# Quads of expert rows loaded and stored in 4 KB runs, and four shared units moved behind quads 5, 11, 17 and 23

## The reference

```
probs = softmax(x2 @ router_w + router_b)            # 64 experts
w, e  = top 8 of probs, weights divided by their sum
moe   = sum over k of w[k] * (silu(x2 @ w1[e[k]] + b1[e[k]]) @ w2[e[k]] + b2[e[k]])
share = sum over 2 shared experts of silu(x2 @ sw1 + sb1) @ sw2 + sb2
out   = layernorm(x2 + moe + share)
```

## Time and profile before

| | before |
|---|---|
| median of 3 runs | 1846.71 us |
| profiled execution: time, span | 1847.5 us, 1845.4 us |
| TensorE busy, mean granted clock | 88%, 0.94 of full |
| VectorE, ScalarE, GpSimd busy | 63%, 34%, 49% |
| chain that ended last | PE 61%, DVE 11%, POOL 11%, DMA 6% |
| quads in the trace | first load issued at 591.6 us, last store issued by 1023.9 us |
| transfers of a quad, time to landing | load 5.8 us, store 4.5 us (medians of 80) |

### The profile page before, as it was taken

How to read it: one execution, slowest core, us unless ns; L and a number is a source line. 1 busy time by engine, 2 the same in 40 slices (tenths; PEclk the granted TensorE clock), 3 DMA queues, 4 the chain that set the end, 5 groups by cost and what they waited for, 6 DMA issues and landing times.

```text
span 1845.4 us, 45541 instructions
## 1 busy us (share of the span) xinstructions
PE 1623.4 (88%) x17739; PEld 1302.6 (71%) x17739; DVE 1165.2 (63%) x3228; ACT 627.1 (34%) x957; POOL 897.3 (49%) x1000
## 2 busy tenths in 40 slices
PE   6898988887898999989998689899882999999994
PEld 5676767776665666766776457677662999999994
DVE  4577777776511776775567578888762445565564
ACT  1233333232311774545554344445421111111110
POOL 0007777777782008888888776533334003223223
PEclk9999999997999999999998799999985999999997
DMA  9516656556688898888889632211315113333332
GB/s 328 183 39 213 218 189 206 178 195 207 203 242 231 280 314 264 286 290 282 294 287 325 238 99 86 82 59 65 122 50 193 53 51 92 93 95 95 95 101 66
DMA packets 269202, 322.41 MB, mean 175 GB/s; under 512 B 25035, under 2 KB 245055, under 8 KB 268223
## 3 DMA queue, kind: packets, MB, share of 16 engines
q1 hardware_dynamic: 232671, 226.01, 38.6%
q0 software_dynamic: 33024, 92.32, 15.4%
q10 hardware_dynamic: 3296, 1.17, 0.3%
HBM read 157.02 MB, written 162.40 MB: 173 GB/s over the span
## 4 chain that ended last, share of the span: by engine, by line
PE 61%; DVE 11%; POOL 11%; DMA 6%; issue 5%; ACT 4%; SPq 1%; DVEq 0%; POOLq 0%; ACTq 0%
PE wide L2147 14%; PE d_yp L2159 7%; POOL big L1509 7%; PE wide L110 4%; PE wide L127 3%; PE wide L1261 3%; PE bank L1095 3%; PE bank L1281 3%; PE wide L1264 2%; PE wide L1248 2%; DMA e_x<-lists 2%; POOL rest_ones L253 2%; PE e_yp L1815 2%; PE bank L1274 2%; ACT pt L746 2%
## 5 line engine op out<-in xcount | busy, mean ns | idle before, releaser
L1509 POOL DMA_INDIRECT big<-results,slots x256 | 266.8, 1042 | 197.9 <-DMA results<-e_y 121.6
L2147 PE MATMUL wide<-d_xt,d_ws 128*128 128x128 f32 x2272 | 278.0, 276 | 0.6 <-issue 0.6
L2147 PEld LDWEIGHTS wide<-d_xt,d_ws 128*128 128x128 f32 x2272 | 271.7, 193 | 4.5 <-issue 1.0
L680 POOL DMA_INDIRECT lists<-big,slots x160 | 157.9, 987 | 84.5 <-DVE slots L1035 38.6
L746 ACT ACTIVATE pt<-wide 77x2048 f32<-77x2048 f32 x64 | 119.7, 1871 | 132.7 <-PE wide L1264 132.2
L2047 ACT ACTIVATE d_gate<-wide 128x512 f32<-128x512 f32 x71 | 42.4, 597 | 326.0 <-PE wide L2147 326.0
L2012 POOL DMA_INDIRECT d_picked<-results,slots x64 | 63.0, 984 | 179.6 <-DMA results<-d_y 166.4
L1524 DVE SCALAR_TENSOR_TENSOR big<-big,weights 128x256 f32<-128x256 f32 x256 | 111.0, 495 | 42.7 <-DMA big<-results,slots 25.3
L110 PE MATMUL wide<-shared_sx,shared_sw 128*128 128x512 f32 x256 | 127.7, 622 | 7.3 <-DMA shared_sx<-res_t 4.9
L2159 PE MATMUL d_yp<-d_wd,d_h 128*128 x568 | 134.2, 379 | 0.0
L127 PEld LDWEIGHTS wide<-shared_sw,shared_sh 128*128 128x128 f32 x512 | 98.8, 194 | 45.7 <-issue 30.1
(11 more groups left out here) (289 smaller groups left out, 3327.4 us busy)
## 6 DMA issues: line engine op xcount, KB each, us to landing
lists<-zero SPq DMA_DIRECT2D x20, 2048.0 KB, 14.7
e_x<-lists SPq DMA_DIRECT2D x80, 512.0 KB, 5.8
results<-e_y SPq DMA_DIRECT2D x80, 512.0 KB, 4.5
d_x<-lists SPq DMA_DIRECT2D x71, 128.0 KB, 2.2
results<-d_y SPq DMA_DIRECT2D x71, 128.0 KB, 1.7
e_w<-in_L_w SPq DMA_DIRECT2D x2, 4096.0 KB, 40.0
shared_sw<-in_x_t SPq DMA_DIRECT2D x32, 128.0 KB
x<-in_x SPq DMA_DIRECT2D x8, 512.0 KB
```

The lines of the kernel that those rows point to most:

```text
L680: pool.indirect_dma_start(out=lists, out_offset=bass.IndirectOffsetOnAxis(ap=slots[:, b, i, k:k + 1], axis=0), in_=z2[i % 3][:, b, :], in_ ...
L1509: pool.indirect_dma_start(out=picked[:, c % NG, b, :], out_offset=None, in_=results[0:-(-PAGES_OF_STEP[s] // 4) * 4 * R0, :], in_offset=ba ...
L2147: ins = mm(out[T % 2][:, a * P:(a + 1) * P], ws[:, T % NW, n, c, a * P:(a + 1) * P], xt[:, T % 2, c], start=c == 0, stop=c == KC - 1)
```

## The change

Three edits. First, `rows_of` lays a quad out so that partition p holds four rows that are neighbours in memory: one run of 4 KB in place of four of 1 KB. For that the integer places are permuted inside each quad, in five more small VectorE operations per step; the float places are kept in `weights` (whose values for the step are written only later), so `slot` and `slots_f` fall away. Second, 16 units instead of 20 stand ahead of the first quad (units 8 to 23). Third, units 24, 25, 26 and 27 follow one each behind quads 5, 11, 17 and 23. `PLANNED` counts the operations of a plan that lost one.

```diff
-        slot = sb("slot", [P, NB, K])
+        slot = None if first else sb("slot", [P, NB, K])
+        row = sb("row", [P, 3, NB, K], mybir.dt.uint32) if first else None
...
                         for b in range(NB):
-                            ins = nc.vector.max(slot[:, b], place[:, b])
+                            ins = nc.vector.max(weights[:, b, i, :], place[:, b])
                         step(ins)
+                        step(nc.vector.tensor_copy(row[:, 0], weights[:, :, i, :]))
+                        nc.vector.tensor_scalar(row[:, 1], row[:, 0], R - 1, 2, ALU.bitwise_and, ALU.logical_shift_left)
+                        nc.vector.tensor_scalar(row[:, 2], row[:, 0], 7, 3, ALU.logical_shift_right, ALU.bitwise_and)
+                        step(nc.vector.tensor_scalar(row[:, 0], row[:, 0], 9, 9, ALU.logical_shift_right, ALU.logical_shift_left))
+                        step(nc.vector.tensor_tensor(row[:, 1], row[:, 1], row[:, 2], ALU.bitwise_or))
+                        nc.vector.tensor_tensor(slots[:, :, i, :], row[:, 0], row[:, 1], ALU.bitwise_or).then_inc(slot_done, 1)
...
-                    nc.vector.tensor_copy(slots[:, :, i, :], slot[:]).then_inc(slot_done, 1)
+                        nc.vector.tensor_copy(slots[:, :, i, :], slot[:]).then_inc(slot_done, 1)
...
-FIRST_UNITS = 20
+FIRST_UNITS = 16
...
         if j < begun:
             if j:
                 weights(1)
-            units(0)
+            units(1 if j % 6 == 5 else 0)
...
-        slots_f = sb("slots_f", [P, NB, STEPS, K0])
...
-        PLANNED = 8
+        PLANNED = 7
...
-            return dram[4 * j * R0:4 * (j + 1) * R0, :].rearrange("(h a p) n -> p h a n", h=2, a=2)
+            return dram[4 * j * R0:4 * (j + 1) * R0, :].rearrange("(p h a) n -> p h a n", h=2, a=2)
...
-            work(nc.vector.tensor_copy(slots_f[:], slots[:]))
...
-                                                      slots_f[:, pair, s].unsqueeze(3).broadcast_to([P, 2, K0, E0]),
+                                                      weights[:, pair, s].unsqueeze(3).broadcast_to([P, 2, K0, E0]),
```

## The result

The kernel after took 1859.68 us (median of 6 runs, 1854.09 to 1865.04) beside 1845.81 us for the kernel before (6 runs, 1842.26 to 1849.41): ratio 1.0071, 95% interval 1.0052 to 1.009. Run again beside experiments it took 1856.64 us (12 runs) against 1848.15: 1.0052, interval 1.0034 to 1.007. It is slower by 8.5 to 14 us, as forecast in direction; the forecast of 1854 us was 3 to 6 us low. The first median lies inside the stated range of 1842 to 1862 us and just above the 1849 to 1859 us of the likeliest case. The profiled execution is the fastest of the six, 1854.09 us, with a span of 1851.2 us; that it falls on the forecast is chance (see the part on the prediction). Lines are shifted: `rows_in` is L1797, `inward` L1809, `outward` L1820, the gathers L1515, the load and store of a quad L1578 and L1582, the send L1591 with the load of rows L1587.

What follows compares the result with a forecast made beforehand. From quad 24 on GpSimd's gathers were taken as the bound, starting once quad 23 is stored. Terms -10.3 + 1.7 + 3.5 + 4.6 + 1.7 + 10.5 - 4.0 + 0.8 - 1.0 = +7.5 us gave 1854 us, range 1842 to 1862.

Steps and rivals of the forecast that it cites:

- the likeliest case: The forecast's own case for the whole kernel, the summed terms: 1854 us, range 1849 to 1859, chance 0.62.
- Start of quad 0: SyncE issues quad 0's load earlier, as unit 24 and its send no longer stand ahead of it: -10.28 us.
- Clock: TensorE idles 11.7 us ahead of quad 0, then runs at 1.2 GHz for some 4 us: +1.7 us.
- Unit 24: Unit 24 now stands behind quad 5 on TensorE and adds its own time there: +3.5 us.
- The send and the half clock behind it: SyncE stands for step 2's send behind quad 6, making quad 10's load late, +4.6 us; TensorE's half clock follows, +1.7.
- Units 25 to 27: Three units ahead of `outward(23)` add 10.5 us on TensorE, of which 4.0 hide in its waits for loads.
- `rank`: Five more VectorE operations per step, showing only in the last step ahead of the rows' addition: +0.8 us.
- Runs of 4 KB: Quad loads in longer runs take 17% less time between quad 10's load and `inward(9)`: -1.0 us, other bound 0.
- the send was not free: Rival: three buffers carry TensorE over SyncE's wait at the send, so +1.2 us in all, 1848 us; chance 0.17.
- The gathers did not get faster: Rival: 4 KB runs relieve the DMA engines and GpSimd's gathers shorten, up to 15.9 us less, 1838 us; chance 0.14.
- VectorE waited longer for gathers: Rival: gathers of 1 KB rows land later behind 4 KB runs, up to +20 us, 1866 us; chance 0.07.
- The runs were joined: Rival: runs not joined, SyncE's queue keeps 232671 packets and the 4 KB term is 0: 1855 us, no separate chance.

Runs made afterwards that it cites:

- e10: e7 with a unit behind six of seven quads after quad 24, not eleven of twelve, and sums behind seven of eight, not six of seven; ratio 0.9948.
- e6: Kernel after without the four units among quads 0 to 23, which go behind quad 24 instead; ratio 1.0017.
- e7: e6 with SyncE sending step 1's rows behind the quads' first loads and loading step 2's rows behind the store of quad 3; ratio 1.0011.
- e5: Kernel after with 80 spare transposes on TensorE ahead of quad 0, which nothing reads; ratio 1.0015.
- e3: Kernel after with SyncE's load of step 3's base rows moved from behind the send to behind the store of quad 9; ratio 1.0044.
- e1: Kernel after with 20 units ahead of quad 0 again and none behind quads 5, 11, 17 and 23; ratio 1.0013.
- e2: Kernel before with 16 units ahead of quad 0 and one each behind quads 5, 11, 17 and 23, runs still 1 KB; ratio 1.0050.
- e4: Kernel after with 52 spare transposes on TensorE ahead of quad 0, which nothing reads; ratio 1.0019.
- e11: e10 with 34 spare transposes on TensorE between the last unit and quad 0; ratio 0.9936.

## Why the prediction was right

The frame held: GpSimd stands until quad 23 is stored, and the moment of its first gather decides. In the sums of the table against the ratios, 8.9 to 12.3 us later is the kernel after, and in e10 12.4 us earlier is 9.6 us off the time. Where this broke (e6, e7) a wait of GpSimd behind the first gather made the difference. One execution follows the frame only roughly: the profiled one of the kernel after has its first gather 9.7 us later than the profiled one before, but took 3.9 us less from there to its end, so its 1854.09 us meets the forecast by luck; the medians are the fair comparison.

- *Start of quad 0*, -10.3: from the last scatter 13.19 instead of 22.40, -9.2. The end of the send's landing sets it in both, and the scatters' landing comes 5.5 us ahead of that (e7), as argued.
- *Clock*, +1.7: mis-sized. From quad 0's first transposes to its store are 11.85 us (584.64 to 596.49) instead of 8.88, and 8.86 in e5, which removes the half clock: 3.0 us. Load to store took 2.65 us more; the load landed a little sooner.
- *Unit 24*, +3.5: the stretch from store 4 to store 5 takes 6.61 instead of 3.11 us, 3.50. From store 0 to store 4 some of it came back: 0 to 5 is 2.8 and 3.2 us longer.
- *The send and the half clock behind it*, 4.6 + 1.7 = +6.3: 8.5 and 5.6 us in the two profiles from store 5 to store 9. SyncE stood for 5.65 and 4.34 us. The two parts can be read apart: TensorE's idle time there grew from 1.98 us to 8.51 and 6.28, +6.5 and +4.3 for the 4.6, and three groups at the lower clock cost 2.0 and 1.4 us for the 1.7. So the mechanism and the size are right. What the sum had not is that the half clock stays when most of the wait goes: in e3 the wait is +1.4 us and the half clock 2.6, so only 1.7 to 4.6 us hang on the standing.
- *Units 25 to 27*, 10.5 - 4.0 = +6.5: 7.1 and 6.5 us from store 9 to store 23; without them (e6) 0.5.
- *`rank`*, +0.8: below what the runs can tell. The end of the attention differs by several microseconds from execution to execution.
- *Runs of 4 KB*, -1.0: 0.45 to 0.68 us less in each of the last three stretches of e1 (one execution), but no faster time in e1 (1.0013), nor in the kernel after beside e2 (1.0071 and 1.0052 against 1.0050). The bound of 0 was the better value. That is what the Trainium skill's rule gave ("DMA: Bandwidth & Descriptors", section Specifications: full rate from 512 B on), though not for its reason: the queue's packets took 38.6% of 1845.4 us and take 37.0% of 1844.4 us in e1 for the same bytes, 29.9 us less on each of 16 engines. So the transfers took less of the DMA engines' time, but the loads' median landing was no shorter (6.0 us against 5.8), and the path doesn't hang on the engines' time.

Without `rank`, which lies ahead of the last scatter, the sum is +6.7 us, against 8.9 and 12.3 from the last scatter to the first gather. It is short by 1.1 us at the start of quad 0, by 0.9 us from its load to its store, by the runs' gain of 1.0 us that can't be seen, and in the first profile by a slower send (8.5 instead of 6.3). Most of these errors lie on one side, so the forecast did not come near by errors that cancel; the range was wide enough for them.

The rivals: the send was not free (a wait of 6.3 to 8.5 us ahead of quad 10). The gathers did not get faster (1060 ns). VectorE waited longer for gathers in the first profile, 32.4 us, but 22.6 in the second, and GpSimd lost nothing by it; the Trainium skill's rule that a DMA engine changes queues only after a whole packet ("DMA: Bandwidth & Descriptors", section Queues, rings and completion order) left no mark that these runs could show. The runs were joined.

## What to carry to other kernels

When a later engine waits for a milestone once, cost a move by what lies between here and the milestone: work shifted inside that stretch is not removed, and only work taken behind it pays, as long as it is spaced so that the engine doing it reaches every later job in time. A load that must wait for a store's landing belongs where nothing urgent stands behind it in the same in-order walk (e3: a wait of 3.35 us instead of 8.51 or 6.28, though no faster time). A hole in TensorE's work cost more than its length here, as the next groups ran at the lower clock (1.94 us instead of 1.06 behind 9.01 us of idling), so look at what the freed engine does in the time won.

## What the runs showed that I had not expected

The half clock ahead of quad 0 does not follow the length of the idle time alone. Idle times of 2.33 us (e1), 3.01 us (e4) and 0.61 us (e11) ahead of quad 0's first transposes, each with 1.28 to 1.29 us more behind them, were followed by groups at half clock; 1.05 us and 1.29 us in the kernel before were not, nor 1.29 us alone in e5. The second group of transposes in the kernel before:

```profile
599.12 1.06 PE L1792 MATMUL e_xp<-ident,e_x 128*128 128x128 f32 x8 [1.29 <-ACT e_xt L1657]
```

In e11 and e4 spare transposes lay ahead, in the kernel before units with wider tiles; which difference counts, the runs don't tell.
